# Attention and FP4 feed-forward layer on one core: wider transfers between the SBUF and the row tiles, maxima split on GpSimd, other places for the 128-row work

## The reference

```python
# attention, on the layer norm of x
x_h = x.reshape(b, t, h, d).transpose(0, 2, 1, 3)
xw = jnp.einsum('bhtd,hde->bhte', x_h, w_att_val)
att = jnp.einsum('bhte,bhse->bhts', xw, x_h) / sqrt(d)
att = jax.nn.softmax(att, axis=-1)
vx = x @ wv_w.T + wv_b
o = jnp.einsum('bhts,bhsd->bhtd', att, vx)
return o @ out_w.T + out_b
# feed-forward, on the layer norm of the sum
gate = fp4_linear(x, w_gate)
y = fp4_linear(x, w_up)
h = jax.nn.silu(gate) * y
return fp4_linear(h, w_down)
```

## Time and profile before

| | |
|---|---|
| median of the runs | 1744.99 us |
| profiled execution | 1744.46 us, of which the span of the trace is 1742.7 us |
| PE busy | 1525.8 us, 88% |
| DVE busy | 1343.5 us, 77% |
| ACT, POOL busy | 866.4 us, 605.2 us |
| DMA | 127.34 MB, mean 73 GB/s |
| granted clock of PE, mean over the span | 0.931 of full speed |
| attention block | SP's first issue in it is at 55.24 us, its first key scores at 89.43 us |

### The profile page before, as it was taken

How to read it: one execution, slowest core, us unless ns; L and a number is a source line. 1 busy time by engine, 2 the same in 40 slices (tenths; PEclk the granted TensorE clock), 3 DMA queues, 4 the chain that set the end, 5 groups by cost and what they waited for, 6 DMA issues and landing times. The chain is left out here.

```text
span 1742.7 us, 34245 instructions
## 1 busy us (share of the span) xinstructions
PE 1525.8 (88%) x8874; PEld 928.7 (53%) x8874; DVE 1343.5 (77%) x2731; ACT 866.4 (50%) x1778; POOL 605.2 (35%) x740
## 2 busy tenths in 40 slices
PE   3388888888898888888888989878999999999998
PEld 3144445455444454454454444445666666666666
DVE  7577676676686776766766857728999999999995
ACT  2056565565665655655656647653333333333332
POOL 2124324333333343243333332213334433333332
PEclk8589999998998998998999989998999999999999
DMA  4523343333343333333343333300000000000000
GB/s 153 147 75 106 105 111 98 101 100 106 93 111 92 107 100 99 110 98 105 100 102 98 110 89 97 113 2 3 19 15 15 15 15 15 15 15 15 15 18 18
DMA packets 82531, 127.34 MB, mean 73 GB/s; under 512 B 28864, under 2 KB 48448, under 8 KB 82368
## 3 DMA queue, kind: packets, MB, share of 16 engines
q1 hardware_dynamic: 74720, 119.55, 23.9%
q10 hardware_dynamic: 7776, 7.36, 1.4%
HBM read 81.67 MB, written 45.15 MB: 73 GB/s over the span
## 5 line engine op out<-in xcount | busy, mean ns | idle before, releaser
L1071 DVE TENSOR_REDUCE neg_max<-ring 128x1 f32<-128x512 f32 x1024 | 649.8, 679 | 212.8 <-PE ring L865 210.9
L1002 ACT ACTIVATE probs<-scores 128x512 f32<-128x512 f32 x1024 | 528.6, 604 | 273.5 <-PE scores L876 273.4
L865 PE MATMUL ring<-x_stack,q_stack 64*128 64x512 f32 x1024 | 247.3, 480 | 127.3 <-DVE o_rows L1123 49.4
L1408 PE MATMUL gu_bank<-splits,f_x_T 128*128 128x352 f32 x1024 | 317.4, 464 | 2.1 <-ACT f_x_T L1386 2.1
L892 PE MATMUL ring<-probs,v_quad 128*32 128x512 f32 x2048 | 279.6, 668 | 1.6 <-DVE o_rows L1123 0.8
L865 PEld LDWEIGHTS ring<-x_stack,q_stack 64*128 64x128 f32 x1024 | 103.3, 197 | 299.9 <-DVE neg_max L1071 152.6
L873 PE MATMUL scores<-q_stack,x_stack 64*128 64x512 f32 x1024 | 216.2, 417 | 36.4 <-DMA max_stack<-max_rows 35.9
L1408 PEld LDWEIGHTS gu_bank<-splits,f_x_T 128*128 128x128 f32 x1024 | 191.6, 192 | 99.3 <-issue 3.0
L723 POOL TENSOR_TENSOR pv_rows<-pv_more,pv_rows 128x512 f32<-128x512 f32 x64 | 82.2, 1284 | 422.3 <-ACT pv_more L1008 420.9
L876 PE MATMUL scores<-max_stack,max_ones 64*128 64x512 f32 x1024 | 211.4, 407 | 0.0
L1236 POOL TENSOR_TENSOR f_rstd<-f_mean_var,eps 128x1 f32<-128x1 f32 x64 | 44.7, 699 | 330.7 <-DVE f_mean_var L1346 330.7
(11 more groups left out here) (130 smaller groups left out, 2102.3 us busy)
## 6 DMA issues: line engine op xcount, KB each, us to landing
q_stack<-q_split SPq DMA_DIRECT2D x512, 64.0 KB, 2.4
x_stack<-x_split SPq DMA_DIRECT2D x256, 128.0 KB, 2.7
x_split<-splits SPq DMA_DIRECT2D x64, 256.0 KB, 2.2
q_split<-splits SPq DMA_DIRECT2D x64, 256.0 KB, 2.3
out_dram<-x_all SPq DMA_DIRECT2D x64, 128.0 KB, 1.7
x_all<-in_L_attn_x_dram ACTq DMA_DIRECT2D x14, 512.0 KB, 5.5
max_rows<-max_turned SPq DMA_DIRECT2D x256, 4.0 KB, 1.8
max_stack<-max_rows SPq DMA_DIRECT2D x128, 8.0 KB
```

The source lines that it names most:

```text
L865: pe.matmul(bank(tiles[m])[:, :], row_tile(q_stack[q], m)[:, p, s * P:(s + 1) * P], row_tile(x_stack[q], m)[:, p, :], start=True, stop=Tru ...
L1002: act.activation(probs[j][:, k, :], scores[k][:, :], ACT.Exp).then_inc(p_ready, 1)
L1071: dve.tensor_reduce(neg_max[g % 2][:, at:at + 1], tile[:, :], AX.X, ALU.max, negate=True).then_inc(m_used, 1)
L1408: m = pe.matmul(gu_bank[c][:, :], x_T[u][:, a, :], gate_up_T[:, a, c * CH:(c + 1) * CH], start=(a == 0), stop=(a == HALVES - 1))
```

## The change

- The split parts are stored in the order in which the row tiles hold them: `x_rows` has all four parts (so x is stored 4 times for each half in place of 2), `q_rows` two. The query tile now holds high, low, high, low and the x tile high, low, low, high, which gives the same four products. A row tile is loaded by one DMA: x from 64 rows of DRAM, q from 32 rows of DRAM through a source that begins with a repeated dimension of 2. SP issues 4 DMAs for a quad's stacks in place of 12. One pair of semaphores, `stored0` and `stored1`, counts all six stores of a half.
- The maxima are stored by one DMA in place of four. Its DRAM side is 4 x 32 x 32 elements.
- POOL splits the maxima (`split_maxima`), in step 0 of the quad before; DVE only turns them, after the fourth maximum of that step in place of the third.
- POOL's order is another (`POOL_STEP`): the values of quad 1 are spread in quad 0, those of quad 2 in (1, 1), those of quad 3 in (2, 0).
- The 128-row work has other places (`IN_STEP`), and DVE's statistics too (`STATS`).

```diff
-    x_split = dram("x_split", [B, HALVES, 2, D, HH, T], F32)
-    q_split = dram("q_split", [B, HALVES, 2, D, HH, T], F32)
+    x_rows = dram("x_rows", [B, HALVES, 4, D, HH, T], F32)
+    q_rows = dram("q_rows", [B, HALVES, 2, D, HH, T], F32)
...
-    IN_STEP = {(0, 1): ("x0",), (0, 3): ("rows3", "q0"), (1, 1): ("turn0", "rows0"), (1, 3): ("turn1",),
-               (2, 1): ("proj0", "x1"), (2, 3): ("q1", "v0", "rows1"), (3, 1): ("proj1",), (3, 3): ("rows2", "v1")}
+    IN_STEP = {(0, 1): ("x0", "rows3"), (0, 3): ("q0", "turn1", "turn0"), (1, 1): ("rows0",), (1, 3): ("proj0",),
+               (2, 1): ("proj1", "x1"), (2, 3): ("rows1", "q1"), (3, 1): ("v0",), (3, 3): ("rows2", "v1")}
...
-    STATS = [(0, 1), (1, 0), (1, 2), (2, 0)]
+    STATS = [(0, 2), (0, 3), (1, 2), (2, 0)]
...
-    POOL_STEP = {(0, 0): ("values",), (0, 1): ("halves", "x0"), (0, 3): ("q0",),
...
+    POOL_STEP = {(0, 0): ("values0", "maxima", "values1", "halves"), (0, 1): ("x0",), (0, 3): ("q0",),
...
+            def split_maxima(i, g, start):
+                u, n = g % 2, QUAD * TT
+                pool.wait_ge(m_used, n * (i + 1))
+                if not start:
+                    pool.wait_ge(m_turned, i - 1)
+                pool.tensor_tensor(max_cols[u][:, 0:n].bitcast(F32R), neg_max[u][:, :],
+                                   one[:, :].broadcast_to([P, n]), ALU.mult).then_inc(m_split, 1)
+                pool.wait_ge(m_split, i + 1)
+                pool.tensor_tensor(max_cols[u][:, n:2 * n].bitcast(F32R), neg_max[u][:, :],
+                                   max_cols[u][:, 0:n], ALU.subtract).then_inc(m_low, 1)
...
-                sp.wait_ge(x_stored[a], 32 * (b + 1))
-                sp.wait_ge(q_stored[a], 32 * (b + 1))
+                sp.wait_ge(stored[a], STORES * (b + 1))
                 for m in range(ROWS):
                     h = h0 + PAIRS * m
-                    for k in range(4):
-                        src = q_split[bass.ds(b, 1), a, k // 2, :, h:h + PAIRS, :]
-                        sp.dma_start(row_tile(q_stack[g], m)[D * k:D * k + D, :, :].bitcast(F32),
-                                     src.rearrange("o d h t -> (o d) h t")).then_inc(stack_loaded[g], 16)
-                    for k in range(2):
-                        src = x_split[bass.ds(b, 1), a, :, :, h:h + PAIRS, :]
-                        sp.dma_start(row_tile(x_stack[g], m)[2 * D * k:2 * D * k + 2 * D, :, :].bitcast(F32),
-                                     src.rearrange("o l d h t -> (o l d) h t")).then_inc(stack_loaded[g], 16)
+                    src = x_rows[bass.ds(b, 1), a, :, :, h:h + PAIRS, :]
+                    sp.dma_start(row_tile(x_stack[g], m).bitcast(F32),
+                                 src.rearrange("o k d h t -> (o k d) h t")).then_inc(stack_loaded[g], 16)
+                    src = q_rows[bass.ds(b, 1), a, :, :, h:h + PAIRS, :].rearrange("o k d h t -> (o k d) (h t)")
+                    sp.dma_start(row_tile(q_stack[g], m).bitcast(F32),
+                                 src.unsqueeze(0).broadcast_to([2, 2 * D, PAIRS * T])).then_inc(stack_loaded[g], 16)
...
+                store(c, a, x_rows, f"x{a}", (xh, xl, xl, xh))
+                store(c, a, q_rows, f"q{a}", (qh, ql))
...
                 sp.wait_ge(m_turned, i + 1)
-                for r in range(TT):
-                    sp.dma_start(max_rows[bass.ds(i, 1), :, r, :].rearrange("o c t -> (o c) t"),
-                                 max_turned[g % 2][32 * r:32 * r + 32, :]).then_inc(max_stored, 16)
-                sp.wait_ge(max_stored, 16 * TT * (i + 1))
+                sp.dma_start(max_rows[bass.ds(i, 1)].rearrange("o c r t -> (o r) c t"), max_turned[g % 2][:, :])\
+                  .then_inc(max_stored, 16)
+                sp.wait_ge(max_stored, 16 * (i + 1))
...
-                        if j == 0 and s < 3 and turning:
-                            max_part(s, i + 1, (g + 1) % QUADS, first and g == 0)
+                        if j == 0 and s == 3 and turning:
+                            turn_maxima(i + 1, (g + 1) % QUADS, first and g == 0)
```

More of the change, by code:

```diff
@@ L173, in first_block @@
                           "qh_done"))
-    x_stored, q_stored = ([sems[f"{n}_stored{a}"] for a in range(HALVES)] for n in "xq")
+    stored = [sems[f"stored{a}"] for a in range(HALVES)]
     x_first, gu_loaded, dn_loaded, vw_loaded, ow_loaded, qw_loaded, bias_loaded, kept = (
@@ L223, in load_x, with store @@
                              x[at:at + n].rearrange("b (s p) e -> p (b s) e", p=P)).then_inc(loaded, 16)
-            def store(a, dst, high, low, stored):
-                for k, t in enumerate((high, low)):
+            def store(a, dst, rows):
+                for k, t in enumerate(rows):
                     sp.dma_start(dst[0:1, a, k].rearrange("o d h t -> (o d h) t"), t[:, a, :].bitcast(F32))\
@@ L243, in _ @@
                 sp.wait_ge(xl_done, a + 1)
-                store(a, x_split, xh, xl, x_stored)
+                store(a, x_rows, (xh, xl, xl, xh))
             for a in range(HALVES):
                 sp.wait_ge(ql_done, a + 1)
-                store(a, q_split, qh, ql, q_stored)
+                store(a, q_rows, (qh, ql))
             for c, (r, n) in enumerate(GU_CHUNKS):
@@ L257, in _ @@
             for a in range(HALVES):
-                sp.wait_ge(x_stored[a], 32)
-                sp.wait_ge(q_stored[a], 32)
+                sp.wait_ge(stored[a], STORES)
             sp.wait_ge(kept, 16 * (len(GU_CHUNKS) + 2))
@@ L538, in attention_block @@
                           "qh_done"))
-    x_stored, q_stored = ([sems[f"{n}_stored{a}"] for a in range(HALVES)] for n in "xq")
+    stored = [sems[f"stored{a}"] for a in range(HALVES)]
     x_loaded, ffn_loaded = sem("x_loaded"), sem("ffn_loaded")
-    STACK = ROWS * 6 * 16
+    STACK = ROWS * 2 * 16
     pool_set, v_spread = sem("pool_set"), sem("v_spread")
@@ L650, in prepared @@
         return not isinstance(c, int) or c < B
-    STATS = [(0, 1), (1, 0), (1, 2), (2, 0)]
+    STATS = [(0, 2), (0, 3), (1, 2), (2, 0)]
     AGGREGATE = (2, 1)
-    POOL_STEP = {(0, 0): ("values",), (0, 1): ("halves", "x0"), (0, 3): ("q0",),
-                 (1, 0): ("values",), (1, 1): ("halves",),
-                 (2, 0): ("values",), (2, 1): ("halves", "x1"), (2, 2): ("deviation",), (2, 3): ("q1",),
-                 (3, 0): ("normal0", "values"), (3, 1): ("halves", "normal1"), (3, 2): ("normal2",),
-                 (3, 3): ("normal3",)}
+    POOL_STEP = {(0, 0): ("values0", "maxima", "values1", "halves"), (0, 1): ("x0",), (0, 3): ("q0",),
+                 (1, 0): ("maxima",), (1, 1): ("halves", "values2"), (2, 0): ("values3", "maxima"),
+                 (2, 2): ("deviation",), (2, 3): ("halves", "x1", "q1"), (3, 0): ("maxima", "normal0"),
+                 (3, 1): ("normal1",), (3, 2): ("halves", "normal2"), (3, 3): ("normal3",)}
     ZEROED = 2
@@ L728, in split @@
                 a = int(kind[1])
[L729 to L731 removed]
+                at, high, low, high_done, low_done = (
+                    (raw[0], xh, xl, xh_done, x_low) if kind[0] == "x" else
+                    (raw[1], qh, ql, qh_done, q_low))
                 pool.wait_ge(kept_used, use(kind, b, BY_ACT) + 1)
[L733 removed]
+                pool.wait_ge(stored[a], STORES * (b + 1))
                 pool.tensor_tensor(high[:, a, :], at[:, :], one[:, :].broadcast_to([P, T]), ALU.mult).then_inc(high_done, 1)
@@ L754, in batch @@
                 first = isinstance(b, int) and b == 0
+                last = isinstance(b, int) and b == B - 1
                 for g in range(QUADS):
@@ L757, in batch @@
                         for task in POOL_STEP.get((g, j), ()):
-                            if task == "values":
-                                ready_values(b, g, first)
+                            if task == "maxima":
+                                if not (last and g == 3):
+                                    split_maxima(QUADS * b + g + 1, (g + 1) % QUADS, first and g == 0)
+                            elif task[:6] == "values":
+                                ready_values(b, int(task[6]), first)
                             elif task == "halves":
@@ L1072, in reduce_max, with turn_maxima @@
                                   AX.X, ALU.max, negate=True).then_inc(m_used, 1)
[L1076 to L1091 removed]
+            def turn_maxima(i, g, start):
+                dve.wait_ge(m_low, i + 1)
+                if not start:
+                    dve.wait_ge(max_stored, 16 * (i - 1))
+                dve.transpose(max_turned[g % 2][:, :], max_cols[g % 2][:, :]).then_inc(m_turned, 1)
             def statistics(d, tiles):
@@ L1171, in _ @@
                 if g == 0:
-                    for part in range(3):
-                        max_part(part, g, g, True)
+                    turn_maxima(g, g, True)
             batch(0)
```

40 lines of the change are left out of this document (10 added, 30 removed).

## The result

| | kernel before | changed kernel |
|---|---|---|
| median (lowest to highest) | 1745.17 us (1744.09 to 1745.71) | 2010.55 us (2004.5 to 2016.09) |
| ratio, 95% interval | | 1.1521 [1.1486, 1.1556] |
| profiled span | 1742.7 us | 2014.2 us |
| granted clock, mean | 0.931 | 0.878 |
| a batch in the middle | 68.27 us | 84.35 us |

The changed kernel is 265.4 us slower; 1922 was forecast, within 1790 to 2100. The two last rows of the table carry the loss: 15 x (84.35 - 68.27) = 241 us and 111.97 - 89.43 = 22.5, together 264.

The account below looks back on a forecast made before the run. PE, the busiest engine, bounds the kernel, with stalls for maxima and values; the new load would make it wait on a DMA chain. 1744.5 + 156 (15 batches) + 20.5 (start) + 1 (last batch) = 1922 us, range 1790 to 2100.

Parts of the forecast that it names:

- Engines of the query load: The repeated-source query load runs on 2 engines, 32 rows of 4 KB on each, instead of 16 engines.
- Ahead of the chain, quad 0: From quad 0's key scores to the stacks' issue: 12.2 us work, 2.5 slow clock, 3.2 and 2.8; sum 20.7 us.
- two stores more of x, hidden by waiting for q0's split: On SP, the additional x stores take 0.9 us but cost nothing, since SP waits for POOL's q split anyway.
- The chain: From the stacks' issue to PE's start on the maxima: 1.0 + 12.2 + 2.0 + 0.4 + 2.3 = 17.9 us.
- the small rows of the maxima: The maxima store's 32 rows per engine, behind the stacks, take 2.0 us; bounds 0.3 (10 ns each) and 2.0.
- The price of a row: Time per stack row on one engine: bounds 0.16 and 0.23 us, 0.17 taken; 72 rows a quad make 12.2 us.
- Quad 2: Work, slow clock and stores before the stacks' issue take 22.2 us, then 17.9 us until PE starts on the maxima.
- The start: All 16 first stack DMAs issued at once; 288 rows per engine put key scores at 109.9, not 89.43: + 20.5 us.
- The place of PE's wait: PE waits for the maxima about 30 times, 6 to 9 us each, over 200 us in sum.
- The other signs: SP waits 12 us or so for the maxima store; DVE's values wait goes; DMA share falls; clock below 0.93.
- the lowest bound: Rows at 0.16 us, no slow clock, 0.3 for the maxima's rows: batch 68.9, + 10 and + 14, 1769 us.
- the two stalls of the old batch "and their wake": In the old batch, PE's waits for maxima and DVE, with slower running afterwards, make 12 us of the 68.27.

Follow-up runs that it names:

- experiment 3: Changed kernel with q stored in four parts with one-row gaps between them, one load per query tile with outermost dimension 4; 1860.42 us.
- experiment 1: Changed kernel with each query tile loaded by two DMAs of 32 rows instead of one with a repeated source; 1600.75 us.
- experiment 2: Changed kernel with q stored in all four parts and each query tile loaded by one DMA of 64 rows without repetition; 1648.43 us.
- experiment 5: Kernel before with each query tile loaded by one DMA through the repeated source, and x loaded by four DMAs; 2040.69 us.
- Experiment 7: Changed kernel with ACT's load of `x_all` moved to quad 1 and DVE's statistics one to three steps later; 1997.68 us.
- experiment 4: Changed kernel with the transfers of before (12 stack loads, four maxima stores, x stored twice), keeping the new places and POOL's work; 1691.62 us.
- experiment 8: Changed kernel with two 32-row DMAs per query tile, and the places, POOL's order and statistics of before put back; 1700.82 us.
- experiment 10: Changed kernel with two 32-row DMAs per query tile and each quad's maxima stored by four DMAs instead of one; 1631.18 us.
- experiment 9: Changed kernel with two 32-row DMAs per query tile and the maxima of even quads stored ahead of the stacks; 1567.47 us.
- experiment 6: Changed kernel with q stored in four parts as two pairs with a gap, so the load begins with 2 without repetition; 2032.73 us.

## Why the prediction was right, and where its sizes were off

**Engines of the query load: right.** The step on which the sign hung was the count of packets of two loads of the maxima, carried over from 2 rows to 64. The DMA view of the changed kernel shows 2.03 engines, experiment 3 moves the count to 4 and the time with it, and experiments 1 and 2 bring 16 engines and the old order of magnitude. In experiment 5 this load alone costs more than the whole change.

**The size.** The forecast loss was 177 us, the measured one 265. Nearly all that is missing is in the batch, 78.7 us forecast and 84.35 measured, 5.65 x 15 = 85 us; the parts follow.

**Ahead of the chain, quad 0: 20.7 forecast, 555.00 - 531.91 = 23.1 measured.** The failing term is "two stores more of x, hidden by waiting for q0's split". POOL ended that split at 548.44 + 1.26 = 549.70 us:

```profile
548.44 1.26 POOL L746 TENSOR_TENSOR splits<-raw_q,splits 128x512 fp32r<-128x512 f32 x1
...
549.95 0.22 POOL L713 TENSOR_TENSOR max_cols<-neg_max,max_cols 128x16 fp32r<-128x16 f32 x1
```

SP had been held by the maxima of quad 1 until 548.15, issued the four x stores from 549.48, and came to q only at 551.64, 1.9 us after POOL. Another 0.5 came from q's stores to the stacks (3.36 us, 2.84 assumed). The cover was computed for an SP that waits; this SP was late itself, because of the very chain that the step before had lengthened. The new work of POOL (two operations of 0.22 us, 0.25 assumed) cost nothing.

**The chain: 17.9 forecast, 573.80 - 555.00 = 18.8 measured.** Its terms, from the trace's packets: first packet 1.3 us after the issue (1.0 assumed); the 72 rows of the later engine from 556.3 to 570.7, 14.3 us or 0.20 us a row (0.17 assumed, 12.2); the small rows of the maxima end at 571.0, 0.3 us later (2.0 assumed); to the issue of the load at 571.52 0.5 (0.4); to PE 2.28 (2.3). The 32 small rows went back to back at about 10 ns, the lower bound of the prediction; what the earlier trace rows showed for three packets was the time in which they came, not a price of each. The two wrong prices nearly cancel, and that is luck. The price of a row should have been taken from the middle of its bounds, 0.16 and 0.23, not near the lower: with two engines at work it was 0.18 us from 564 to 570 us (12.7% of 16 engines over 6 us for 69 rows), yet not on average over the chain.

**Quad 2: 22.2 + 17.9 forecast, 21.9 + 20.6 measured** (573.80 to 595.66 to 616.26). Of the 2.7 us more in the chain, 0.9 can be put down to the prices that were off in quad 0 already, and the other 1.8 to ACT's load of `x_all`, which the forecast priced in no chain: 512 KB in rows of 1 KB, which, if they are on all engines, are also on the pair. Beside such a load, from 517 to 523 us:

```profile
q10 hardware_dynamic: 462, 0.46, 34.5%
q1 hardware_dynamic: 45, 0.17, 12.7%
```

SP's queue (q1) moved 45 packets, against 72 in the same 6 us alone, and ACT's load took 11.4 us in the median where it took 5.5. Experiment 7 confirms the place: without it that chain lost 2.7 us in the mean.

The batch in sum: 78.7 forecast + 2.4 + 0.9 - 0.3 + 2.7 = 84.4. **The start**, + 20.5 forecast, was + 22.5.

**The place of PE's wait.** Forecast were about 30 waits for the maxima of 6 to 9 us. There are two a batch, of that size (277.7 us in 38), but they end with the query tile, and the maxima add a second wait of 1.7 to 2 us. The forecast let PE wait at the last link, while the same queue delays the link before it. That one half would not be hidden (30 waits, not 15) was right. The other signs came as said: SP's wait (12 us forecast, 11.7 measured), no wait for values, a clock below 0.93 (0.878), and the mean share of SP's DMA queue down from 23.9 to 20.8%:

```profile
q1 hardware_dynamic: 70112, 136.28, 20.8%
```

One sign is weaker than it was said to be: the query loads have no landing time in the table of issues, but since they share a semaphore with x's, which run on all engines, these have lost theirs too.

**Two slips in the working.** In the lowest bound the start comes to 20.5 - 2.9 - 1.7 = 15.9 us, not 14, so that bound is 1771. And the 12 us put down to the two stalls of the old batch "and their wake" are 2.52 + 3.37 + 1.65 + 2.13 = 9.7 by its own rows; the other 2.3 stay open. Neither moves the forecast.

**What the change would have been worth.** Its good parts were real: the value stall went (experiment 4), and the transfers, once spread, are worth 44 us alone (experiment 8), the joined store of the maxima 30 of the kernel of experiment 1 (experiment 10). With the query load in two pieces the change is 8% faster than before, with the maxima stored early 10%.

**Expectations that missed.** Experiments 3 and 5 were expected 110 and 76 us too low, 2 showed the doubled stores at 48 instead of at most 30, 7 gave back 13 of 30, and 9 gained 33 where 21 were expected. In 2, 3, 5 and 9 the direct term was summed and what follows on SP and in the clock was not; how much of each it was is not separated.

## What to carry to other kernels

Before several small DMAs are joined, look at the outermost dimension of both sides of the joined one: a leading repeated 2 put 64 rows of 4 KB on two of 16 engines and the whole change cost 15%; with two DMAs of 32 rows it gained 8%. A short outermost dimension on the DRAM side alone was enough (experiments 3 and 6), with nothing repeated. Read the width in the DMA view over a stretch in which that transfer is alone: 12.7% of 16 engines is two engines. And look at what stands behind the narrow transfer on its queue: the loss was paid by the small stores and loads that followed it, so what is urgent is to be issued ahead of what is long. In experiment 9, where the loads were spread already, that gave 33 us.

## What was not expected of the hardware

SP's issue itself stalls while the pair has many rows outstanding. SP at the start of the changed kernel's attention block:

```profile
57.30 0.90 SPq L803 DMA_DIRECT2D x_stack<-x_rows  x1
...
58.84 5.96 SPq L803 DMA_DIRECT2D x_stack<-x_rows  x1
...
90.74 4.72 SPq L823 DMA_DIRECT2D max_rows<-max_turned  x1
```

The first DMAs of the stacks are issued in 0.5 to 0.9 us; from the seventh on each of those for x takes 4.8 to 6.0 us, about the time of the 32 rows that a query load leaves on an engine (32 x 0.18). The forecast let all 16 be issued at once. It cost little here (+ 22.5 us for + 20.5), presumably because the pair had rows to move all the while.

The number of outstanding rows on an engine seems to be what stops the issue. No run was made for it, but three on record vary it. With 4 engines (experiment 3) the issue first stops at the eleventh DMA:

```profile
60.82 4.46 SPq L803 DMA_DIRECT2D x_stack<-x_rows  x1
```

Before that stop each of the 4 engines had been given 5 x 16 rows of q and 5 x 4 of x, 100 rows. Before the stop at the seventh DMA above, and at the seventh in experiment 6, each of the two had been given 3 x 32 and 3 x 4, 108 rows. With 16 engines (experiment 1) all 16 tiles put 8 x 4 + 8 x 4 = 64 rows on an engine, and from the third tile on every DMA was issued in about 0.5 us (one pair of the first query tile took 3.1). So the stop came with some 100 rows given to an engine, fewer outstanding by what had moved, and did not come at 64. Whether it is rows that are counted, and at what number, no run settles.
